# A mixture of experts' tile loop: inputs two tiles ahead, the result copied by another engine, expert numbers loaded one by one

## The reference

```python
top_vals, top_idx = jax.lax.top_k(x @ router_w.T, 2)
weights = jax.nn.softmax(top_vals, axis=-1)
hid = jax.nn.silu(x @ wg) * (x @ wu)      # of each expert: 128 -> 256
y = hid @ wd                              # 256 -> 128
acc + ce[:, None] * y
```

## Time and profile before

| what | us |
|---|---|
| median of three runs | 4312.42 |
| lowest and highest of them | 4293.04, 4312.71 |
| span of the profiled execution (first to last instruction) | 4303.2 |
| the experts' stage, first to last gate matmul | about 1685 to 2075 |
| TensorE, VectorE, ScalarE, POOL busy over the span | 3438.5, 3076.0, 1871.6, 1093.0 |

### The profile page before, as it was taken

How to read it: one execution, slowest core, us unless ns; L and a number is a source line. 1 busy time by engine, 2 the same in 40 slices (tenths; PEclk the granted TensorE clock), 3 DMA queues, 4 the chain that set the end, 5 groups by cost and what they waited for, 6 DMA issues and landing times. The chain is left out here.

```text
span 4303.2 us, 131223 instructions
## 1 busy us (share of the span) xinstructions
PE 3438.5 (80%) x54119; PEld 2128.0 (49%) x54119; DVE 3076.0 (71%) x7658; ACT 1871.6 (43%) x4392; POOL 1093.0 (25%) x1947
## 2 busy tenths in 40 slices
PE   5999999997779622777557999999868999999519
PEld 1222222221357511444425778887547788877404
DVE  7777777773856641333567899999778999998377
ACT  1556555565244201222435665555346665554200
POOL 1000111100000274333104554332226543332000
PEclk6999999998889756999757999999859999999559
DMA  6022222200000111111210000000000000000118
GB/s 136 13 39 51 51 51 51 51 5 9 0 1 1 74 51 41 46 50 47 91 53 8 14 9 9 9 9 6 5 7 10 9 14 9 4 9 6 47 50 304
DMA packets 98607, 155.93 MB, mean 36 GB/s; under 512 B 17060, under 2 KB 60969, under 8 KB 97728
## 3 DMA queue, kind: packets, MB, share of 16 engines
q1 hardware_dynamic: 83776, 120.28, 10.8%
q0 software_dynamic: 13088, 23.06, 1.8%
q10 hardware_dynamic: 1152, 4.19, 0.2%
HBM read 103.21 MB, written 45.30 MB: 35 GB/s over the span
## 5 line engine op out<-in xcount | busy, mean ns | idle before, releaser
L2055 ACT ACTIVATE s_E<-s_Y,s_M 128x9 f32<-128x9 f32 (+38 forms) x2048 | 656.5, 392 | 626.4 <-DVE s_M L1968 624.2
L343 DVE TENSOR_REDUCE half_max<-bm 128x1 f32<-128x512 f32 x1024 | 653.2, 684 | 228.8 <-PE bm L264 224.2
L1869 PE MATMUL g_x<-s_ik,s_iqm 128*32 128x1 f32 (+63 forms) x16384 | 673.7, 280 | 25.3 <-DVE g_o L1951 11.6
L455 ACT ACTIVATE E<-sc 128x1024 f32<-128x1024 f32 x512 | 521.0, 1024 | 358.9 <-PE sc L278 348.1
L1963 DVE SCALAR_TENSOR_TENSOR s_Y<-s_Y,g_x 128x9 f32<-128x9 f32 (+38 forms) x2048 | 576.4, 281 | 47.3 <-PE g_x L1869 1.2
L1881 PE MATMUL g_p<-mats,s_E 128*128 128x128 f32 x3072 | 450.0, 284 | 43.2 <-ACT s_E L2055 39.5
L264 PE MATMUL bm<-ks,qs 96*128 96x512 bf16 x1024 | 416.3, 409 | 74.7 <-DVE half_max L343 43.8
L1869 PEld LDWEIGHTS g_x<-s_ik,s_iqm 128*32 128x32 f32 x16384 | 392.3, 116 | 151.1 <-issue 74.8
L1881 PEld LDWEIGHTS g_p<-mats,s_E 128*128 128x128 f32 x3072 | 340.2, 144 | 110.7 <-ACT s_E L2055 65.7
L264 PEld LDWEIGHTS bm<-ks,qs 96*128 96x128 bf16 x1024 | 99.2, 97 | 551.1 <-DVE half_max L343 455.5
L1968 DVE TENSOR_REDUCE s_M<-s_Y 128x4 f32<-128x8 f32 (+56 forms) x512 | 350.8, 685 | 0.2
(11 more groups left out here) (353 smaller groups left out, 5155.2 us busy)
## 6 DMA issues: line engine op xcount, KB each, us to landing
e_spread<-d_gate SPq DMA_DIRECT2D x64, 512.0 KB, 6.1
d_parts<-parts SPq DMA_DIRECT2D x8, 1536.0 KB, 5.9
qs<-d_parts SPq DMA_DIRECT2D x96, 128.0 KB, 8.4
ks<-d_parts SPq DMA_DIRECT2D x96, 128.0 KB, 12.2
me_xg<-d_xs SPq DMA_DIRECT2D x144, 65.0 KB, 1.8
mc_yb<-d_ys SPq DMA_DIRECT2D x8, 1024.0 KB, 5.5
resid<-in_x SPq DMA_DIRECT2D x8, 512.0 KB, 8.3
rden<-d_den POOLq DMA_DIRECT2D x16, 256.0 KB, 3.8
```

The costliest lines, as they stand in the source:

```text
L343: dve.tensor_reduce(half_max[n // SETS % 2][:, idx // 2, idx % 2:idx % 2 + 1], bm[n % 2][:, :], AX_X, ALU.max).then_inc(max_done, 1)
L455: act.activation(E[:, G % 2, h, :], sc[n % 2][:, :], ACT.Exp, scale=0.25).then_inc(exp_done, 1)
L1869: mm = pe.matmul(x_ps[u % 3][32 * b:32 * (b + 1), rho % 2, 0:n + 1], iqm[n // WINDOW % 2][:, b, x0:x0 + D, :], s.ik[:, b, rho, 0:n + 1], s ...
L2055: act.activation(E[:, m % 2, rho, 0:m + 1], Y[:, D * (m % YR) + rho, 1:2 + m], ACT.Exp, bias=M[:, D - 1 + D * m + rho:D + D * m + rho]).th ...
```

## The change

It does three things. The input of a tile is transposed and copied two tiles ahead, no longer one; VectorE makes that copy in front of the product of the present tile, and `xT` has three buffers. The copy of the result out of PSUM goes from VectorE to ScalarE. TensorE's sequencer loads one expert number for each tile, right behind the gate matmul of the tile before. Beside these, `XR` goes from 6 to 8, and SP loads row numbers for 4 tiles at a time (`GROUP` 4, which now concerns SP alone).

```diff
-        XR, YR, GROUP = 6, 6, 16
+    XR, YR, GROUP = 8, 6, 4
-        xT = [sb(f"xT{i}", [P, P]) for i in range(2)]
+        xT = [sb(f"xT{i}", [P, P]) for i in range(3)]
...
+                def expert_of(n):
+                    return nc.values_load_multi_w_load_instructions(
+                        m.expert[0:1, n:n + 1], engines=(mybir.EngineType.PE,), min_val=0, max_val=NE - 1)[1][0]
...
-                experts = []
+                experts = {0: expert_of(0)}
                 turn(0)
+                turn(1)
                 for n in range(TILES + 2):
-                    if n % GROUP == 0 and n < TILES:
-                        experts = experts[-2:] + list(nc.values_load_multi_w_load_instructions(
-                            m.expert[0:1, n:n + GROUP], engines=(mybir.EngineType.PE,), min_val=0, max_val=NE - 1)[1])
-                        head = n - len(experts) + GROUP
                     if n < TILES:
-                        gate_up_mm(n, experts[n - head])
+                        gate_up_mm(n, experts[n])
                     if n + 1 < TILES:
-                        turn(n + 1)
+                        experts[n + 1] = expert_of(n + 1)
+                    if n + 2 < TILES:
+                        turn(n + 2)
                     if 1 <= n <= TILES:
                         turn_hidden(n - 1)
                     if n >= 2:
-                        down_mm(n - 2, experts[n - 2 - head])
+                        down_mm(n - 2, experts.pop(n - 2))
...
                 def copy_in(n):
                     dve.wait_ge(turned, n + 1)
-                    if n >= 2:
-                        dve.wait_ge(mm_g, n - 1)
-                    dve.tensor_copy(xT[n % 2][:, :], xT_ps[n % 2][:, 0:P]).then_inc(x_out, 1)
+                    if n >= 3:
+                        dve.wait_ge(mm_g, n - 2)
+                    dve.tensor_copy(xT[n % 3][:, :], xT_ps[n % 2][:, 0:P]).then_inc(x_out, 1)
...
                 copy_in(0)
-                for n in range(TILES + 2):
-                    if n < TILES:
-                        gated(n)
-                    if n + 1 < TILES:
-                        copy_in(n + 1)
-                    if n >= 2:
-                        address(n - 2)
-                        copy_out(n - 2)
+                copy_in(1)
+                for n in range(TILES):
+                    if n + 2 < TILES:
+                        copy_in(n + 2)
+                    gated(n)
+                    address(n)
...
+                def copy_out(n):
+                    act.wait_ge(mm_d, n + 1)
+                    if n >= YR:
+                        act.wait_ge(y_sent[n % YR], 16 * (n // YR))
+                    act.activation(y[n % YR][:, :], y_ps[n % 2][:, 0:P], ACT.Copy).then_inc(y_out, 1)
+
-                for n in range(TILES + 1):
+                for n in range(TILES + 2):
                     if n < TILES:
                         silu_gate(n)
-                    if n:
+                    if 1 <= n <= TILES:
                         copy_hidden(n - 1)
+                    if n >= 2:
+                        copy_out(n - 2)
```

More of the change, by code:

```diff
@@ L1436, in gate_up_mm @@
                         pe.wait_ge(hid_done, n - 1)
-                    pe.matmul(gu_ps[n % 2][:, :], xT[n % 2][:, :], m.w_gu[:, bass.ds(expert * (2 * FF), 2 * FF)],
+                    pe.matmul(gu_ps[n % 2][:, :], xT[n % 3][:, :], m.w_gu[:, bass.ds(expert * (2 * FF), 2 * FF)],
                               start=True, stop=True).then_inc(mm_g, 1)
@@ L1494, in gated @@
                                       ).then_inc(hid_done, 1)
[L1496 to L1500, removed]
-                copy_in(0)
-                for n in range(TILES + 2):
-                    if n < TILES:
-                        gated(n)
-                    if n + 1 < TILES:
-                        copy_in(n + 1)
-                    if n >= 2:
-                        address(n - 2)
-                        copy_out(n - 2)
+                copy_in(0)
+                copy_in(1)
[4 more added lines that the diff above has]
+                    address(n)
             @block.scalar
```

## The result

| | before | changed |
|---|---|---|
| median of four runs, us | 4307.6 | 4134.1 |
| lowest and highest | 4293.0, 4312.7 | 4123.2, 4147.6 |
| span of the profiled execution | 4303.2 | 4140.4 |
| first to last gate operation | 390.3 | 233.4 |

A fourth run of the kernel before, 4302.8 us, has joined the three of the first table. The ratio of the times is 0.9608 (95% interval 0.9581 to 0.9635): 3.9% faster. That is outside the forecast range, on the fast side: 4181 was forecast, 4155 was the lowest allowed.

A forecast was written before the change was run, and what follows sets the result against it. Bound: the 2.34 us loop through the input copy, plus pauses at each sixteenth tile. Stage 390.3 to 267.6 us saves 122.7, the start 8.5; 4312.4 - 131.2 = 4181 us, range 4155 to 4258.

The forecast's parts named there:

- What bounds the kernel: Experts stage: a 2.34 us loop a tile through gate, SiLU, product and input copy, plus 46 us of load pauses.
- TensorE's own work: TensorE per tile without waits: gate 0.96 plus 7 x 0.11 = 1.73 us, taken as 1.75.
- The load of one number: TensorE's sequencer, each tile: one expert number taken at 0.6 us, between 0.07 and 1.10; round 1.85 us.
- 1.25: TensorE's sequencer: microseconds a round takes without the load itself, with issue, the check pair and the gap behind the load.
- priced by the word: TensorE's sequencer: a load under 0.5 us leaves TensorE's 1.75 us a tile to decide; 4167 us, chance 0.14.
- The 3 us for rounds at the low clock: Start of the experts stage: the first three rounds stay at the low clock, each 0.9 us over 2.34.
- The base: Whole time: runs' median 4312.42 us lies 9.2 above the profiled span 4303.2, a difference set on both sides alike.
- The start: Before the first gate: SP's shorter checks save 3.5 us, TensorE's moved first load the rest; together 8.5 us.
- ScalarE's copy: Result copy, 144 times, moved from VectorE to ScalarE: 0.33 us each, zero on the path.
- The product behind the copy: VectorE: product behind copy n+2 ends about 2.2 us after its gate, wanted about 3.2 after; 1 us of cover.
- The fixed price: TensorE's sequencer: one number costs 1.10 us like sixteen, round 2.35 us; 4253 us, chance 0.28.
- The load that waits: TensorE's sequencer: load starts only when the gate matmul ahead has ended; 4413 us, or 4341 at 0.6; chance 0.05.

The follow-up runs named there:

- the first experiment: The changed kernel with TensorE's sequencer again loading 16 expert numbers in front of each sixteenth gate matmul: 4208.5 us, ratio 0.9781.

## Why the prediction was wrong

*What bounds the kernel* was right: the loop through the input copy, and the pauses at each sixteenth tile. Both are gone in the changed profile: the single loads alone removed what the eight pauses and the start cost (52.6 us), and the rest came from the copy. What failed are the sizes of the two terms that come next, the load and TensorE's own work.

*The load of one number* failed first. I took 0.6 us, halfway between the ends 0.07 and 1.10, because the upper end would make fifteen further words free. It measured 0.386; four such words together cost no more than one, and a row of before could not show that. With 1.25 + 0.39 = 1.64 the sequencer's round is not the bound that the forecast made of it. By the sum's own rule, the longer of the two rounds, the right load alone would have put TensorE's 1.75 in the place of 1.85 and the stage at 253.3, which is 14 of the 34 us that the stage's forecast of 267.6 lacked. The Trainium skill (DMA: Bandwidth & Descriptors, section Latency and other measured facts) has a floor of about 600 ns; the 144 loads at 0.297 to 0.495 us contradict it, and the measurement decides.

*TensorE's own work* failed next, and it set the lower end of the range. 1.73 us came from a tile that had idled before its gate, whose 0.96 us hold 0.10 in which the weights went in with nothing beside them. Packed, the tile takes 0.86 + 7 x 0.11 = 1.63, so the rival "priced by the word" at 4167 was itself 143 x 0.12 = 17 us too slow, and no case reached the measured time. The 3 us for rounds at the low clock were too many as well: the first two steps of the changed kernel took 1.92 and 1.41 us, with fewer passes in them than a full tile has. So the 34 us are 14 for the load, 17 for TensorE's work and 3 for the first rounds.

*The base* took a share. The forecast put 9.2 us between span and run's time. The profiled run of the changed kernel has 1.8 (4142.2 against 4140.4), so the span of before stood for a run of about 4305, not 4312. That is 7 of the 47 us between the forecast 4181 and the measured 4134; another 8 are that the profiled run of the changed kernel was slower than the median of its four.

*The start* was right: 8.5 forecast, 9.2 measured. The single loads alone, with SP still in groups of 16, bring the first gate from 13.6 to 8.5 us behind SP's first load (1671.1 to 1679.6). With SP in groups of four and TensorE's loads in groups of 16 it stands 10.3 us behind (1659.4 to 1669.7 in the first experiment). So TensorE's load is worth 5.1 us alone and SP's shorter groups 3.3, where 5.0 and 3.5 were forecast. SP's longer ring was not tried apart. *ScalarE's copy* at nothing on the path was right (0.277 us against 0.33, and moving it back changed nothing). *The product behind the copy* had its cover, as forecast, and the 0.29 us for a check with its assertion was right.

*The rivals.* The fixed price: not so, since sixteen cost 1.10 and one 0.386, but four aligned numbers do cost as one. By the word: right for pairs and off the fourths, about 0.25 us a number. The Trainium skill (Runtime: NRT & Kernel Launch, section Instruction fetch mechanics) has about 200 ns a register, and goes on to speak of the loads that the runtime puts in. The loads here come from SBUF: off the fourths, at 0.25 us, they are near that figure, while sixteen aligned numbers, an estimated 3.2 us by it, took 1.10. The load that waits: what spoke for it is real, a waiting matmul ahead holds a load. But the gate's waits sit on the register operation, so here nothing ahead waits, and the loads did not wait for passes: one ran at 1802.7 for 0.358 us, while the gate ahead of it started only at 1803.23. The range had no case below 4155 because its lowest case took TensorE's work too long, kept the 3 us for the first rounds and took the higher base.

## What to carry to other kernels

When a wait goes, price the engine that comes next from a stretch in which it is fed without gaps; here a duration taken behind an idle time held 0.10 us of weight load that a full stretch hides. A sequencer's loads, checks and issue are an engine of their own: add up its round and compare it with the array's, since here under 0.1 us a tile decided that 144 small loads beside the work cost nothing, where nine large ones in front of it cost 64 us of the stage. A part of a change that sounds like its core may be worth nothing by itself: here the copy's engine and its place.

## What was not expected of the hardware

- The price of a register load depends on where it begins: 4 numbers 0.398 us at a fourth and 1.01 off it, 8 numbers 0.603 and 2.01, 16 at a sixteenth 1.10. An eight-number load can cost nearly twice a sixteen-number one, and an aligned pair (0.56) more than an aligned four.
- The single load takes about 0.30 us on some kernels and 0.39 on others (medians 0.301 to 0.400 over those with one load a tile); what makes the difference was not tried.
- A load on TensorE's sequencer does not pass a matmul that waits for a semaphore (3.7 us behind SP's, with the transpose's data), but it does pass matmuls that only wait for the array (1802.7, ahead of the gate of 1803.23).
- The check and the assertion of one number, 0.29 us, cost nearly as much as its fetch; a pause of 4.91 us brought two rounds at a granted clock of 0.53, near the 1.2 GHz level, before 1.64 us came back at 1.00.
